# A fused decoder layer: the per-expert constants in one rounded product, and the final addition divided anew between TensorE, VectorE and GpSimd

## The reference, cut to what matters

```python
probs = softmax(xn @ Wr + br)
scores, idx = top_k(probs, 2)
full = relu(xn @ W1_e + b1_e) @ W2_e + b2_e      # for the chosen experts
c = einsum('ef,efh->eh', relu(b1), W2) + b2      # what an expert gives for a row of zeros
c_total = c.sum(axis=0)
output = sum(scores * (full[idx] - c[idx] + c_total), axis=2)
x = layernorm(residual + output)
```

## Time and profile before

| | us |
|---|---|
| median of three runs | 749.09 |
| the profiled execution's own time | 751.12 |
| its span, first to last instruction | 749.4 |
| TensorE busy | 693.6 (93%) |
| VectorE busy | 470.1 (63%) |
| ScalarE busy | 332.7 (44%) |
| GpSimd busy | 257.8 (34%) |

### The profile page before, as it was taken

How to read it: one execution, slowest core, us unless ns; L and a number is a source line. 1 busy time by engine, 2 the same in 40 slices (tenths; PEclk the granted TensorE clock), 3 DMA queues, 4 the chain that set the end, 5 groups by cost and what they waited for, 6 DMA issues and landing times.

```text
span 749.4 us, 14972 instructions
## 1 busy us (share of the span) xinstructions
PE 693.6 (93%) x5014; PEld 597.2 (80%) x5015; DVE 470.1 (63%) x1088; ACT 332.7 (44%) x994; POOL 257.8 (34%) x204
## 2 busy tenths in 40 slices
PE   7699999999999999999788979999999999999984
PEld 7689787888879889897777857888888888878842
DVE  2643536586876778777888765555555555545566
ACT  4566766676676767666632212221222122212203
POOL 1300000120603205042447228477029800077752
PEclk9899999999999999999798779999999999999996
DMA  8458485651002010010514124435324421113333
GB/s 300 118 192 293 143 283 172 221 183 44 30 15 72 15 43 30 16 58 1 184 40 158 50 70 141 155 120 176 98 70 150 142 72 42 42 57 99 114 92 112
DMA packets 68496, 82.66 MB, mean 110 GB/s; under 512 B 5932, under 2 KB 59736, under 8 KB 68440
## 3 DMA queue, kind: packets, MB, share of 16 engines
q1 hardware_dynamic: 59800, 52.54, 21.8%
q0 software_dynamic: 8640, 29.38, 12.2%
HBM read 45.04 MB, written 36.86 MB: 109 GB/s over the span
## 4 chain that ended last, share of the span: by engine, by line
PE 78%; DVE 7%; ACT 7%; POOL 3%; issue 2%; DMA 2%; SPq 0%; ACTq 0%; DVEq 0%; POOLq 0%
PE bank L1047 14%; PE bank L793 8%; PE bank L795 7%; PE bank L794 7%; PE bank L1017 5%; PE bank L1019 5%; PE bank L1018 5%; PE bank L1027 4%; PE bank L915 4%; PE bank L954 4%; PE bank L966 3%; ACT arena L1178 3%; PE bank L974 1%; PE bank L1113 1%; PE bank L1003 1%
## 5 line engine op out<-in xcount | busy, mean ns | idle before, releaser
L1047 PE MATMUL bank<-w_ring,hidT_hi 128*128 (+1 forms) x320 | 119.8, 408 | 3.1 <-DVE hidT_lo L1678 3.1
L1299 ACT ACTIVATE hidT_hi<-bank 128x512 fp32r<-128x512 f32 x80 | 43.5, 596 | 168.1 <-PE bank L1027 168.1
L1178 ACT ACTIVATE arena<-bank,negmx 128x128 f32<-128x128 f32 x256 | 91.0, 378 | 6.5 <-DVE negmx L1340 6.5
L1047 PE MATMUL bank<-w_ring,hidT_lo 128*128 (+1 forms) x320 | 83.3, 281 | 0.0
L1656 DVE TENSOR_TENSOR arena<-bank,b_rep 128x512 f32<-128x512 f32 x80 | 55.4, 692 | 42.8 <-PE bank L1019 42.5
L1662 DVE TENSOR_REDUCE work<-bank 128x256 f32<-128x512 f32 x40 | 27.7, 692 | 77.0 <-PE bank L1047 76.7
L1047 PEld LDWEIGHTS bank<-w_ring,hidT_hi 128*128 128x128 f32 x320 | 60.1, 188 | 14.8 <-issue 3.8
L1017 PE MATMUL bank<-w_ring,xgT_hi 128*128 (+1 forms) x160 | 67.7, 423 | 4.5 <-POOL w_ring L621 1.6
L1019 PE MATMUL bank<-w_ring,xgT_lo 128*128 (+1 forms) x160 | 63.9, 399 | 0.0
L1018 PE MATMUL bank<-w_ring,xgT_hi 128*128 (+1 forms) x160 | 63.5, 397 | 0.0
L1346 DVE RECIPROCAL rinv<-rsum 128x8 f32<-128x8 f32 x32 | 6.5, 203 | 90.6 <-ACT arena L1178 90.5
(11 more groups left out here) (267 smaller groups left out, 1887.6 us busy)
## 6 DMA issues: line engine op xcount, KB each, us to landing
xg_dram<-zeros SPq DMA_DIRECT2D x9, 2176.0 KB, 9.0
w_raw<-in_L_ffn_W_dram POOLq DMA_DIRECT2D x16, 1024.0 KB, 6.4
y_dram<-zeros SPq DMA_DIRECT2D x2, 2560.0 KB, 10.8
work<-xg_dram SPq DMA_DIRECT2D x40, 128.0 KB, 2.1
y_dram<-work SPq DMA_DIRECT2D x40, 128.0 KB, 1.7
b_rep<-in_L_ffn_b_dram POOLq DMA_DIRECT2D x8, 512.0 KB, 4.2
work<-gmax_dram SPq DMA_DIRECT2D x14, 256.0 KB, 3.9
arena<-in_x_dram SPq DMA_DIRECT2D x8, 256.0 KB, 2.7
```

The lines of the kernel that those rows point to most:

```text
L1047: last = pe.matmul(o, l, r, start=c == 0 and l is both[0], stop=c == FC - 1 and l is both[0])
L1178: last = nc.scalar.activation(probs[:, n % 2, h * S:(h + 1) * S], ps_score[:, h * S:(h + 1) * S], ACT.Exp, bias=negmx[:, n % 2, h:h + 1], ...
```

## The change

`constants_in` becomes one float32r product per block. The weights are split into a rounded part and the rest of it (`wgt3` holds rounded, rounded, rest: 24 columns), so that the transposed table has 24 partitions; the constants become a table `c3` of 24 rows (rounded, rest, rounded), so that a product over 24 partitions holds high x high, high x low and low x high. GpSimd makes `wgt3` after the last scatter, and TensorE's first `shares_transposed` waits for it. `b2` is loaded three times, into partitions 0, 8 and 16; the gather of constant rows has 24 rows.

The high rows of the second block of each pair are now added by TensorE, `high_in`: an fp32 product of a diagonal matrix (`diag`, made by GpSimd ahead of the loading of `b2`) with the gathered rows. The second block's result stays in PSUM, where VectorE takes its moments and ScalarE or VectorE normalises it. VectorE's `add_high` does the first block only. `BY_POOL` becomes the eight even blocks, so GpSimd does eight of the additions of low rows and VectorE eight. ScalarE normalises all four blocks of the first three groups of four.

```diff
-        BY_POOL = (0, 2, 4, 6)
+        BY_POOL = range(0, B, 2)
...
+        def added(b):
+            return bank_of(b // 2)[:, D:2 * D] if b % 2 else y_all[:, 0, b, :]
...
             for q in range(QUADS):
-                sp.wait_ge(out_ready, q + 1)
+                if q == QUADS - 1:
+                    sp.wait_ge(out_ready, 1)
                 sp.wait_ge(out_scaled, q + 1)
...
             scatter(Z)
+            for k in range(2):
+                pool.tensor_copy(wgt3[:, :, k, :], wgt[:, :, :]).then_inc(wgt_rounded, 1)
+            pool.wait_ge(wgt_rounded, 2)
+            pool.tensor_tensor(wgt3[:, :, 2, :], wgt[:, :, :], wgt3[:, :, 0, :].bitcast(F32), ALU.subtract)\
+                .then_inc(wgt_split, 1)
...
+            for p in range(PAIRS):
+                pool.tensor_tensor(diag[:, p, :], ident[:, :], share[:, 1, 2 * p + 1:2 * p + 2].broadcast_to([P, P]), ALU.mult)\
+                    .then_inc(diag_ready, 1)
             pool.wait_ge(w_split, 2 * E)
-            pool.dma_start(b2_sb, b2).then_inc(b2_loaded, 16)
+            for k in range(3):
+                pool.dma_start(b2_sb[k * E:(k + 1) * E, :], b2).then_inc(b2_loaded, 16)
...
                 if b - 2 in BY_POOL:
                     add_low(b - 2)
+            add_low(B - 2)
...
             pe.wait_ge(wo_read, 2 * PAIRS)
+            pe.wait_ge(wgt_split, 1)
             shares_transposed(0)
...
             def constants_in(p):
                 for b in (2 * p, 2 * p + 1):
-                    last = pe.matmul(bank_of(p)[:, b % 2 * D:(b % 2 + 1) * D], wgtT[b // 4][:, b % 4 * S:(b % 4 + 1) * S], yz,
-                                     start=False, stop=b % 2 == 1)
-                last.then_inc(part_done, 1)
+                    pe.matmul(bank_of(p)[:, b % 2 * D:(b % 2 + 1) * D], wgtT[b // 4][:, b % 4 * S:(b % 4 + 1) * S], c3,
+                              start=False, stop=False)
+
+            def high_in(p):
+                pe.wait_ge(diag_ready, p + 1)
+                pe.wait_ge(gathered[p], 16 * 2)
+                pe.matmul(bank_of(p)[:, D:2 * D], diag[:, p, :], y_all[:, 1, 2 * p + 1, :], start=False, stop=True)\
+                    .then_inc(part_done, 1)
...
             for p in range(PAIRS):
                 constants_in(p)
+                high_in(p)
                 if p + 3 < PAIRS:
                     low_in(p + 3)
...
-                for b in range(1 if q < QUADS - 1 else 2, 4):
-                    last = nc.scalar.activation(xres[:, 4 * q + b, :], y_all[:, 0, 4 * q + b, :], ACT.Identity,
+                for b in range(0 if q < QUADS - 1 else 2, 4):
+                    last = nc.scalar.activation(xres[:, 4 * q + b, :], added(4 * q + b), ACT.Identity,
...
+                dve.wait_ge(ident_ready, 3)
+                dve.tensor_reduce(of_row[:, :], ident[0:3 * E, 0:3 * E].rearrange("p (k e) -> p e k", k=3), AX.X, ALU.add)
+                chain.link(dve.tensor_reduce(second[:, :], ident[0:3 * E, E:2 * E], AX.X, ALU.add))
+                chain.link(dve.tensor_scalar(second[:, :], second[:, :], -1.0, None, ALU.mult))
...
-            dve.tensor_tensor(yz, b2_sb, bank[2][0:E, 0:D], ALU.add).then_inc(dterm_ready, 1)
+            dve.tensor_tensor(c_hi, b2_sb, bank[2][0:3 * E, 0:D], ALU.add)
+            chain.link(dve.tensor_tensor(yz, b2_sb, bank[2][0:3 * E, 0:D], ALU.add))
+            dve.scalar_tensor_tensor(c3, c_hi.bitcast(F32), second[:, 0:1], yz, ALU.mult, ALU.add).then_inc(dterm_ready, 1)
...
             for q in range(QUADS):
-                for b in range(4 * q, 4 * q + 4):
+                for b in (4 * q, 4 * q + 2):
                     add_high(b)
-                    if b % 4:
-                        dve.wait_ge(high_added, b)
-                        dve.bn_stats(stats4[:, (b - 1) % 4, :], y_all[:, 0, b - 1, :])
-                dve.wait_ge(high_added, 4 * q + 4)
-                chain.link(dve.bn_stats(stats4[:, 3, :], y_all[:, 0, 4 * q + 3, :]))
+                    dve.bn_stats(stats4[:, b % 4 + 1, :], added(b + 1))
+                    dve.wait_ge(high_added, b // 2 + 1)
+                    last = dve.bn_stats(stats4[:, b % 4, :], added(b))
+                chain.link(last)
```

More of the change, by code:

```diff
@@ L191, in decoder_layer @@
         off[0] = 0
-        yz, b2_sb, dterm = [carve(w_raw, D)[0:E, :] for _ in range(3)]
+        yz, b2_sb, dterm = [carve(w_raw, D)[0:3 * E, :] for _ in range(3)]
+        c_hi, c3 = [over(4 * (3 + k) * D, w_raw_at, name, D)[0:3 * E, :] for k, name in enumerate(("c_hi", "c3"))]
+        ctx_aug_at = nc.sbuf_base
         ctx_aug = sb("ctx_aug", [P, 2, 2, KC, AUG])
@@ L204, in decoder_layer @@
         gtok = sb("gtok", [P, 2, 4 * XH])
+        xnT_at = nc.sbuf_base
         xnT = sb("xnT", [P, KC, 2 * S])
@@ L231, in decoder_layer @@
         early = sb("early", [P, 1], I32)
-        zslot_f = sb("zslot_f", [E, 1])
-        zslot = sb("zslot", [E, 1], U32)
+        zslot_f = sb("zslot_f", [3 * E, 1])
+        zslot = sb("zslot", [3 * E, 1], U32)
+        diag = nc.alloc_sbuf_tensor_at("diag", [P, PAIRS * P], F32, offset=wq_lo_at + 4 * RING * F)[:, :]\
+            .rearrange("p (k t) -> p k t", k=PAIRS)
+        of_row = sb("of_row", [3 * E, E])
+        second = sb("second", [3 * E, 1])
         idx = sb("idx", [P, 2, B])
@@ L240, in decoder_layer @@
         shift = sb("shift", [P, E])
-        own = sb("own", [E, E])
+        own = sb("own", [3 * E, E])
         own_row = sb("own_row", [P, 2 * B])
@@ L245, in decoder_layer @@
         tile_end = sb("tile_end", [P, E], I32)
-        wgtT = [ctx_aug[:, k, :, :, :].rearrange("p b c n -> p (b c n)")[0:E, 0:4 * S] for k in range(2)]
-        wgtT += [xnT[:, :, :].rearrange("p c t -> p (c t)")[0:E, :], x1T[1][:, :, :].rearrange("p c t -> p (c t)")[0:E, :]]
+        wgtT = [over(0, at, f"wgtT{g}", 4 * S)[0:3 * E, :]
+                for g, at in enumerate((ctx_aug_at, ctx_aug_at + 16 * S, xnT_at, x1T_at))]
+        wgt3 = xT2[0][:, :, :].rearrange("p c t -> p (c t)")[:, 0:3 * B * E].rearrange("p (b k e) -> p b k e", b=B, k=3)
         gmax_dram = nc.dram_tensor("gmax_dram", [PAIRS, XH, 2 * S], F32, kind="Internal").ap()
@@ L367, in decoder_layer @@
         wgtT_done = sem("wgtT_done")
+        wgt_rounded = sem("wgt_rounded")
+        diag_ready = sem("diag_ready")
+        wgt_split = sem("wgt_split")
         wgtT_copied = sem("wgtT_copied")
@@ L1070, in shares_transposed @@
                 for b in range(4):
-                    last = pe.transpose(bank[7][0:E, b * S:(b + 1) * S], wgt[:, 4 * g + b, :], ident[:, :])
+                    last = pe.transpose(bank[7][0:3 * E, b * S:(b + 1) * S],
+                                        wgt3[:, 4 * g + b, :, :].rearrange("p k e -> p (k e)").bitcast(F32), ident[:, :])
                 last.then_inc(wgtT_done, 1)
@@ L1124, in _ @@
             pe.wait_ge(c_ready, 1)
-            pe.matmul(bank[2][0:E, 0:D], ones[0:E, 0:E], dterm, start=True, stop=True).then_inc(csum_done, 1)
+            pe.matmul(bank[2][0:3 * E, 0:D], ones[0:E, 0:3 * E], dterm[0:E, :], start=True, stop=True).then_inc(csum_done, 1)
             for p in range(3):
@@ L1715, in rows_of_y @@
                 chain.link(dve.tensor_scalar(y_first[:, :], y_first[:, :], float(P), None, ALU.mult))
-                chain.link(dve.tensor_tensor(own[:, :], y_first[0:E, :], ident[0:E, 0:E], ALU.mult))
+                chain.link(dve.tensor_tensor(own[:, :], y_first[0:3 * E, :], of_row[:, :], ALU.mult))
                 chain.link(dve.tensor_reduce(zslot_f[:, :], own[:, :], AX.X, ALU.add))
@@ L1785, in normalise_out @@
                     .then_inc(shift_ready, 1)
-                for b in range(1 if q < QUADS - 1 else 2):
-                    last = dve.tensor_scalar(xres[:, 4 * q + b, :], y_all[:, 0, 4 * q + b, :], mv4[k][:, b, 0:1],
-                                             rstd4[k][:, b:b + 1], ALU.subtract, ALU.mult)
-                last.then_inc(out_ready, 1)
+                if q == QUADS - 1:
+                    for b in range(2):
+                        last = dve.tensor_scalar(xres[:, 4 * q + b, :], added(4 * q + b), mv4[k][:, b, 0:1],
+                                                 rstd4[k][:, b:b + 1], ALU.subtract, ALU.mult)
+                    last.then_inc(out_ready, 1)
             def add_high(b):
@@ L1794, in add_high @@
                 dve.wait_ge(part_done, b // 2 + 1)
-                at = (3, 4, 5, 6, 0, 1, 7, 2)[b // 2] * 512 + b % 2 * D
-                dve.scalar_tensor_tensor(y_all[:, 0, b, :], y_all[:, 1, b, :], share[:, 1, b:b + 1], banks[:, at:at + D],
+                dve.scalar_tensor_tensor(y_all[:, 0, b, :], y_all[:, 1, b, :], share[:, 1, b:b + 1], bank_of(b // 2)[:, 0:D],
                                          ALU.mult, ALU.add).then_inc(high_added, 1)
             dve.wait_ge(z_gathered, 16)
-            dve.wait_ge(b2_loaded, 16)
+            dve.wait_ge(b2_loaded, 48)
             dve.tensor_tensor(dterm, yz, b2_sb, ALU.add).then_inc(c_ready, 1)
```

7 lines of the change are left out of this document (4 added, 3 removed).

## The result

The changed kernel takes 748.14 us in the median of 20 executions (745.54 to 750.86), the kernel before 752.38 in the median of 20 beside it (747.44 to 759.83). The ratio is 0.9943, interval 0.9922 to 0.9963. Forecast were 0.9964 and 746.4 us in a range of 743.8 to 749.9. The time lies inside and it is no change by the measure of 1%. The gain, 4.2 us by the ratio's centre (2.8 to 5.9), is larger than the 2.7 forecast, and the forecast ratio lies just above the interval. A ratio here is computed from all executions, so it need not be the quotient of the two medians.

The account below looks back on a forecast made before the run. TensorE and VectorE run nearly abreast behind the last tile, so both must get cheaper: 3.35 us there, 2.8 after ScalarE, 2.7 taken. 751.12 becomes 748.4 profiled, 746.4 against the median 749.09; range 743.8 to 749.9.

Parts of the forecast that it names:

- TensorE's terms: Behind the last tile: constants 0.24 us a pair, diagonal product 0.53, low product 1.05; a pair's constants and diagonal 0.77.
- the 256-column instructions in those sixteen show no load: Ground for pricing constants by columns: sixteen traced float32r instructions, 0.46 ns a column, so no weight load added to 0.24.
- the rival with weight loads: Short products on TensorE show weight loads, a pair up to 1.59 us instead of 0.77; in part or full, chance 0.13.
- The start of the constants: Unmoved at 724.63 us, behind the third low product; VectorE's table, up to 0.9 later at 723.2, stays hidden.
- VectorE: Behind the last tile: 1.05 us a pair, no surcharge for moments from PSUM, last variance 3.35 us earlier.
- ScalarE and the store: At the end: six normalisations instead of five take 3.07 us, the gain shrinks to 2.8, stores follow as before; 2.7 taken.
- the 1.0 taken for its delay: GpSimd before the first gather: eight products and two loads, mostly hidden in 4.40 us of idle, delay 1.0 us.
- The start of the expert stage: GpSimd brings the rounded weights by 439.2 us, TensorE wants them at 442.92: hidden, 3.7 us of cover.
- the 65 us place: VectorE has three small operations more, 0.6 us, then waits 2.13 for TensorE: nothing taken, 0.6 at worst.
- more gained: Half clock at 720 us missed, by phase or 24 columns in the sum over experts: 1.3 us more, 745, chance 0.13.
- Nothing gained: Short products on TensorE cost their weight loads, pair 1.59 us, variance 1.8 later, about 750; weight loads' chance 0.13.
- The half clock: TensorE stays at 1.2 GHz from 724.6 us on, end 6.6 - 0.5 later, about 755 us; chance 0.04.

Follow-up runs that it names:

- wide: Kernel before with its fp32 constants over 128 partitions instead of 8, zeros below row 8: 774.17 us against 777.29, ratio 0.9951.
- grouped constants: Changed kernel with the constants of two pairs issued together: 754.53 us, ratio to the kernel before 0.9666.
- the lower additions alone: Kernel before with GpSimd adding the eight even lower blocks, VectorE the eight odd: 754.45 us against 750.96, ratio 1.0038.
- four lower blocks on GpSimd: Changed kernel with GpSimd adding four lower blocks, VectorE twelve: 746.94 us, ratio 0.9943; on a chip with standstills 773.85 us, ratio 0.992.
- The one-edit pair: Changed kernel with GpSimd adding four lower blocks, 773.85 us, and the whole change, 758.15 us, on the same chip.

## Why the prediction was right, and where it was not

*The time: inside the range, in part by luck.* The forecast stood on a median of three, 749.09 us; that of 20 beside the changed kernel is 752.38, 3.3 more. The gain was 1.5 larger than forecast. The two errors offset each other, and 748.14 is left where 746.4 was forecast.

*What bounds the kernel: right.* TensorE and VectorE ran abreast. In the stretch behind the first constants the cheap constants alone brought 2.3 us, the diagonals alone lost 3.0, with the fall of the clock in it, both together 2.8.

*TensorE's terms: mis-sized.* The constants of a pair take 0.43 us, not 0.24; diagonal and low product 0.54 and 0.95, together 0.1 less than the 1.58 taken. A pair is 1.92 instead of 1.82, and the last three, for which I took 0.77, are 1.06, exactly what they were before. From the first constants to the last diagonal it is 12.8 us, not 11.4. The step that failed is "the 256-column instructions in those sixteen show no load". They show none, and their neighbours have the same height, 128 partitions. This was the rival with weight loads, in part: 0.2 of its 0.8 us a pair. The runs with wide and with grouped constants show that the load appears where the height changes. In the changed kernel height and number format change together and can't be told apart there; the wide constants show that height alone suffices. A pair with no change of height would be 0.24 + 0.43 + 0.86 = 1.53 us, an estimate from the rows above; the 0.39 above it is two changes, as much as in the kernel before (2.11 - 1.72).

*The start of the constants: nearly.* The table came at 722.25 and TensorE waited 0.23 for it. The cover was the half clock of the low products; at full clock, 2.8 us for three, it is just too short.

*VectorE: right.* 1.06 a pair for 1.05 (734.86 to 735.92). The last variance comes 2.8 us sooner relative to the first constants, not 3.35, since pair 5 starts on VectorE 10.8 us behind them and not 10.1. Moments from PSUM step at 0.35 and from SBUF at 0.32 to 0.34. The Trainium skill ("VectorE: DVE Perf Modes", section "The TRN2 errata — SBUF-src ops pay a fixed extra latency per instruction") has 62 cycles more for VectorE from PSUM, an estimated 65 ns at its 0.96 GHz; the trace shows at most half of that. For ScalarE it has 52 cycles less from PSUM, an estimated 43 ns at its 1.2 GHz, and there the trace agrees: its steps are 0.51 and 0.49 from SBUF and 0.45 from PSUM.

```profile
737.77 0.60 ACT L1367 ACTIVATE xres<-arena,shift,rstd 128x256 f32<-128x256 f32 x1 [0.79 <-DVE shift L1828]
738.28 0.55 ACT L1367 ACTIVATE xres<-bank,shift,rstd 128x256 f32<-128x256 f32 x1
738.73 0.59 ACT L1367 ACTIVATE xres<-arena,shift,rstd 128x256 f32<-128x256 f32 x1
```

*ScalarE and the store: right.* The six normalisations take 2.94 us for 3.07. ScalarE ends 3.04 behind the last variance, 0.4 us more than before, and the store takes as long. The two terms together give 2.4 where I had 2.7.

*GpSimd: covered, as forecast, though the 1.0 taken for its delay was none.* The products took 2.92 (3.0) and the loads 1.62. The first gather starts 5.3 us after the last split in both, so the 4.40 was waiting. The power for blocks 0 to 3 was done at 730.40, VectorE asked for it at 730.9. The start of the expert stage and the 65 us place cost nothing: the rounded weights were ready at 439.4 and wanted at 442.0, the wait of 2.13 is 1.69.

*The rival "more gained": it came true in the profiled execution.* The low products ran at full clock there, 2.81 us for three, and this is the 1.4 us of the first line of the table. Of the two causes named, the 24 columns of the sum over experts are not needed: the kernel with the lower additions alone has 8 columns and full clock (2.81), the one with the constants alone 24 columns and half clock (4.46). So it is the phase or something else that differs between executions. How often either kernel meets the half clock there is not shown, and so neither is its share in the 4.2 us.

*Two prices of rivals don't follow from their own sums.* "Nothing gained" puts the variance 1.8 us later, which with 749.09 makes 750.9, and 751.4 with the fourth normalisation, outside the range and not "about 750". The half clock takes the 0.5 us of that normalisation off where it must be added.

*What was missing: two effects outside the ledger of one trace.* The first is that the alternation with 8-partition products runs at half clock in some executions. I had the hint, 0.64 at 737 us with TensorE busy, and used it only as a danger to the changed kernel, with 0.04. It is a cost of the kernel before: in all four traces with such products the clock falls while TensorE is busy, 3.7, 9, 13 and 16 us behind the first constants, the 13 in the trace shown ahead of the prediction. Of the nine with 24 partitions none has such a fall. What it is worth can only be estimated. 6 of the 20 executions of the kernel before lie above 754 us and raise its mean from 751.2 to 752.7, so 1.5 us. The means of the two kernels are 4.7 apart, and with 2.4 from the ledger this makes 3.9 of them; 0.8 stay open. No gap in the 20 times marks the 754, and no long execution on such a chip was profiled, so that the clock makes them long is argued from the others. Where the mean clock is on record (46 executions of the kernel before on two such chips) it fits: 0.950 to 0.959 in the nine long ones, 0.956 to 0.968 in the rest. The second effect is the standstill on two chips, 23 us of gain that no row of the first trace shows.

## What to carry to other kernels

A short product priced by its columns alone is priced too low where its neighbours have another height: each change of height cost 0.2 us here, because the weight load did not start ahead. Give it the full height with zeros or put several together. When two engines run abreast, price the change for each alone and for both, and look whether the relief of one is bought from the other. And compare executions, not only medians, on more than one chip: what looks like spread can be a mode of the old kernel.

## What the hardware showed that was not expected

- Beside 8-partition fp32 constants in alternation with full-height products TensorE's clock fell to 1.2 GHz without an idle gap in all four traces, early or late. On ordinary chips 15 of 66 executions of such a kernel took 754 us or more, where the median is 750 to 752. With constants of 24 partitions in float32r none did: 0 of 20, 0 of 12 and 0 of 12. On the chips with standstills the upper group is gone with 128 partitions in fp32 (0 of 12) and with four lower blocks on GpSimd (0 of 8). The kernels there with eight lower blocks are few and spread widely (753.7 to 760.2 for the whole change, 6 executions), so they say nothing on it.
- While GpSimd issues indirect gathers, one in 1.26 us, TensorE, VectorE and ScalarE stood still on two chips and not on the others met; it cost 24 us ahead of the first low product. With additions between the gathers, 1.28 and 2.56 us apart in turn, it is gone until the dense part begins. The one-edit pair (773.85 and 758.15 us) shows that this edit is worth 15.7 us there. Through what the engines are held, and why other chips don't show it, stays open; late instruction fetches go with it in two traces (the kernel before and four lower blocks) and not in two others.
- Weight loads started 0.2 us ahead of their product where the product before had the same height, and with it where the height changed. Zeros over 120 more partitions made the alternation of the kernel before 0.4 us a pair faster.
